# Linear attention with a routed MoE on one core: per-head q and k features by folded weights, or from one projection spread by DMA

## The reference

```python
h = _layernorm(x) * (1 + ca) + sa                 # ca, sa: from silu(c) @ wmod, per sequence
qkv = h @ w_qkv.T;  q, k, v = split(qkv)           # to blocks: [b, head, block, 32, 16]
qp = elu(einsum('bhcsd,hdf->bhcsf', q, proj)) + 1.0    # 16 -> 128 features
kp = elu(einsum('bhcsd,hdf->bhcsf', k, proj)) + 1.0
kv = einsum('bhcsf,bhcsd->bhcfd', kp, v)
num = einsum('bhcsf,bhcfd->bhcsd', qp, kv);  ksum = kp.sum(axis=3)
z = 1.0 / (einsum('bhcsf,bhcf->bhcs', qp, ksum) + 1e-08)
x = x + ga * ((num * z) @ w_out.T + b_out)
h = _layernorm(x) * (1 + cb) + sb
x = x + gb * ffn(h)       # best of 8 experts by a small gate: w1 128x512, gelu, w2 512x128, times its score
```

## Time and profile before

| | us |
|---|---|
| median of 3 runs | 293.38 (293.2 to 293.75) |
| profiled execution, first to last instruction | 292.5 |
| begin of the first head's `phi` | 15.3 |
| one steady step | 21.6 |
| last `phi` of the last step done | 189.1 |
| tail behind it | 103.4 |

### The profile page before, as it was taken

One profiled execution on the slowest core, in us unless ns is written; L12 is line 12 of the kernel. 1 busy time (PEld: TensorE's weight loads), 2 busy tenths in 40 slices (PEclk: granted clock), 3 DMA queues, 4 the chain that ended last, 5 costly groups with the idle time before them and its releaser, 6 DMA issues.

```text
span 292.5 us, 11379 instructions
## 1 busy us (share of the span) xinstructions
PE 264.7 (91%) x3952; PEld 212.3 (73%) x3953; DVE 233.8 (80%) x772; ACT 224.2 (77%) x516; POOL 166.2 (57%) x193
## 2 busy tenths in 40 slices
PE   8999799999999999999999999899686999999970
PEld 2566576678778777777777776678575999999960
DVE  3787969989999999999999989988884476676750
ACT  2589698999989989989989988856964667676740
POOL 7004154344476675675685681878788874454551
PEclk9999999999999999999999999999999999999996
DMA  5999800000001001001001011513355344444400
GB/s 149 286 358 300 199 3 2 2 4 4 2 29 56 30 29 56 31 29 57 29 29 56 29 45 70 163 58 113 126 168 176 117 126 123 112 126 131 117 28 0
DMA packets 16239, 26.13 MB, mean 89 GB/s; under 512 B 2608, under 2 KB 11060, under 8 KB 16193
## 3 DMA queue, kind: packets, MB, share of 16 engines
q1 hardware_dynamic: 12896, 17.10, 21.2%
q0 software_dynamic: 3296, 8.41, 8.0%
HBM read 15.32 MB, written 10.64 MB: 89 GB/s over the span
## 4 chain that ended last, share of the span: by engine, by line
PE 45%; DVE 20%; issue 8%; ACT 8%; POOL 5%; DMA 2%; POOLq 1%; ACTq 0%; DVEq 0%; SPq 0%
PE ps L885 9%; DVE phi L1179 8%; PE ps L913 8%; PE ps L810 6%; PE ps L812 4%; PE ps L811 4%; PE ps L821 3%; ACT ebuf L577 3%; ACT ebuf L581 2%; PE ps L843 2%; POOL sorted_rows L458 2%; DVE h L1248 2%; PE ps L835 2%; DVE ln_st L1231 2%; PE ps L879 1%
## 5 line engine op out<-in xcount | busy, mean ns | idle before, releaser
L1179 DVE SCALAR_TENSOR_TENSOR phi<-ps,ebuf 128x512 f32<-128x512 f32 x128 | 81.9, 680 | 13.2 <-ACT ebuf L581 13.1
L577 ACT ACTIVATE ebuf<-ps 128x1024 f32<-128x1024 f32 x64 | 65.5, 1024 | 15.5 <-PE ps L812 15.0
L581 ACT ACTIVATE ebuf<-ebuf 128x512 f32<-128x512 f32 x128 | 74.4, 636 | 0.1
L810 PE MATMUL ps<-hT_hi,mix_lo 128*128 128x512 f32 x128 | 58.4, 456 | 8.1 <-DVE phi L1179 4.5
L635 ACT ACTIVATE gT<-ps,b_cols 128x128 f32<-128x128 f32 x156 | 44.6, 367 | 17.1 <-PE ps L885 14.6
L812 PE MATMUL ps<-hT_hi,mix_hi 128*128 128x512 f32 x128 | 50.6, 396 | 0.0
L811 PE MATMUL ps<-hT_lo,mix_hi 128*128 128x512 f32 x128 | 50.6, 395 | 0.0
L913 PE MATMUL ps<-w_sb,gT 128*128 x312 | 42.3, 278 | 4.0 <-DVE y L1501 2.8
L913 PEld LDWEIGHTS ps<-w_sb,gT 128*128 128x128 f32 x312 | 37.9, 192 | 6.0 <-issue 5.9
L527 POOL DMA_INDIRECT out<-yo,tok x27 | 27.0, 1001 | 23.8 <-DVE yo L1517 21.9
L458 POOL DMA_INDIRECT sorted_rows<-rec,pos x32 | 32.6, 1017 | 8.4 <-issue 6.6
(11 more groups left out here) (208 smaller groups left out, 465.2 us busy)
## 6 DMA issues: line engine op xcount, KB each, us to landing
rin<-sorted_rows SPq DMA_DIRECT2D x39, 192.5 KB, 2.5
w1b<-in_L_ffn_w SPq DMA_DIRECT2D x1, 2048.0 KB, 14.2
sorted_rows<-pad_rec SPq DMA_DIRECT2D x9, 192.5 KB, 6.2
w1b<-in_L_ffn_b SPq DMA_DIRECT2D x1, 512.0 KB, 7.4
sorted_rows<-rec,pos POOLq DMA_INDIRECT x32, 3.1
out<-yo,tok POOLq DMA_INDIRECT x27
wmod_sb<-in_L_wmod SPq DMA_DIRECT2D x1, 384.0 KB, 4.0
x_all<-in_L_attn_x SPq DMA_DIRECT2D x1, 256.0 KB, 3.4
```

Source lines behind the costliest of these rows:

```text
L577: nc.scalar.activation(ebuf[:, h % 2, :, :], x_ps[h % 2], ACT.Relu, scale=-1.0).then_inc(s_neg, 1)
L581: nc.scalar.activation(ebuf[:, h % 2, j, :], ebuf[:, h % 2, j, :], ACT.Exp, scale=-1.0).then_inc(s_exp, 1)
L810: mm(x_ps[h % 2][:, j, :], mix_lo[:, j, h, :], hi, start=True, stop=False)
L1179: v.scalar_tensor_tensor(out=phi[:, h % 4, j, :], in0=x_ps[h % 2][:, j, :], scalar=0.0, in1=ebuf[:, h % 2, j, :], op0=ALU.max, op1=ALU.add ...
```

## The change

q and k of a group are projected once, by two fp32 products of 128 rows (`project`, PE), cast to a high part (`keep_hi`, ACT) and a low part (`split_lo`, now on DVE). Then DMAs on SP's queue (`feed_heads`) lay them out anew in `feed`: under each head its 16 rows of the high, low and again high part, and a row of ones, at partitions 0 to 48 for q and 64 to 112 for k. A head's features are then one product of 49 rows for each of q and k. The row of ones adds 1 to the feature, and everything is scaled by `SHRINK`, so that elu(x)+1 = max(x + 1, min(exp(x), 1)) takes one ACT and one DVE instruction of 1024 columns; the scale is taken out in `keep_a`. `vals` now has the column of ones itself, and four DMAs a group (`spread_values`) write the diagonal blocks of `vbd` instead of DVE. The additions to the variances go to POOL, and the first normalisation runs two groups ahead. The rest of x is loaded in two DMAs, ACT's queue loads `proj` in six; the expert weights are loaded two experts at a time in steps 1 to 4, the pads in step 1, the biases in step 2. The modulation rows are made before the first step. `feed` and `qk` have one buffer each.

```diff
 # SP
+            def feed_heads(g, half, j):
+                sp.wait_ge(s_lo, 2 * g + j + 1)
+                if g:
+                    sp.wait_ge(s_x, H * (g - 1) + HH * (half + 1))
+                for part, row in ((0, 0), (1, HD), (0, 2 * HD)):
+                    sp.dma_start(feed[2 * BLK * j + row:2 * BLK * j + row + HD, HH * half:HH * (half + 1), :].bitcast(F32),
+                                 qk[HH * HD * half:HH * HD * (half + 1), part, j, :].bitcast(F32)).then_inc(s_ld[half][j], 16)
...
+            def spread_values(g):
+                sp.wait_ge(s_vs, g + 1)
+                if g == 0:
+                    sp.wait_ge(c_vbd, 2)
+                else:
+                    sp.wait_ge(s_av, 2 * g)
+                for c in range(NC):
+                    sp.dma_start(vbd[c * BLK:(c + 1) * BLK, c, :],
+                                 vals[c * BLK:(c + 1) * BLK, :, :, :].rearrange("p t h w -> p (t h w)")).then_inc(s_vbd, 16)
...
+            for g in range(NG - 1):
+                if g:
+                    spread_values(g)
+                feed_heads(g + 1, 0, 0)
+                feed_heads(g + 1, 0, 1)
+                if 1 <= g <= E // 2:
+                    load_experts(2 * (g - 1))
+                if g == 1:
+                    sp.wait_ge(c_dve, 1)
+                    for e in range(E + 1):
+                        sp.dma_start(sorted_rows[e * REGION:e * REGION + P, :], pad_rec[:, :]).then_inc(s_tail, 16)
+                if g == 2:
...
+                feed_heads(g + 1, 1, 0)
+                feed_heads(g + 1, 1, 1)
+            spread_values(NG - 1)
 # ACT
-                nc.scalar.activation(ebuf[:, h % 2, :, :], x_ps[h % 2], ACT.Relu, scale=-1.0).then_inc(s_neg, 1)
-                between()
-                act.wait_ge(s_neg, H * g + h + 1)
-                for j in range(2):
-                    nc.scalar.activation(ebuf[:, h % 2, j, :], ebuf[:, h % 2, j, :], ACT.Exp, scale=-1.0).then_inc(s_exp, 1)
+                nc.scalar.activation(ebuf[:, h % 2, :, :], x_ps[h % 2], ACT.Exp, scale=1.0 / SHRINK,
+                                     bias=math.log(SHRINK) - 1.0).then_inc(s_exp, 1)
+
+            def keep_hi(g, j, first=False):
+                act.wait_ge(s_qk, 2 * g + j + 1)
+                if not first:
+                    for half in range(2):
+                        act.wait_ge(s_ld[half][j], 48 * g)
+                nc.scalar.copy(qk[:, 0, j, :], t_ps).then_inc(s_hi, 1)
 # PE
+            def project(g, j):
+                if j == 0:
+                    pe.wait_ge(s_ht, g + 1)
+                else:
+                    pe.wait_ge(s_lo, 2 * g + 1)
...
+                mm(t_ps, wqkT[:, j, :], hT[:, :], start=True, stop=True).then_inc(s_qk, 1)
...
+                for j in range(2):
+                    rows = slice(2 * BLK * j, 2 * BLK * j + 3 * HD + 1)
+                    last = mm(x_ps[h % 2][:, j, :], proj_k[rows, h, :], feed[rows, h, :], start=True, stop=True)
+                last.then_inc(s_x, 1)
 # DVE
+            def split_lo(g, j):
+                dve.wait_ge(s_hi, 2 * g + j + 1)
+                v.tensor_tensor(qk[:, 1, j, :], t_ps, qk[:, 0, j, :].bitcast(F32), ALU.subtract).then_inc(s_lo, 1)
...
-                for j in range(2):
-                    dve.wait_ge(s_exp, 2 * (H * g + h) + j + 1)
-                    v.scalar_tensor_tensor(out=phi[:, h % 4, j, :], in0=x_ps[h % 2][:, j, :], scalar=0.0,
-                                           in1=ebuf[:, h % 2, j, :], op0=ALU.max, op1=ALU.add).then_inc(s_phi, 1)
+                dve.wait_ge(s_exp, H * g + h + 1)
+                v.scalar_tensor_tensor(out=phi[:, h % 4, :, :], in0=ebuf[:, h % 2, :, :], scalar=SHRINK,
+                                       in1=x_ps[h % 2], op0=ALU.min, op1=ALU.max).then_inc(s_phi, 1)
```

## The result

The changed kernel takes 326.75 us (324.75 to 327.43, 4 runs) where the kernel before took 293.29 beside it: a ratio of 1.113, 95% interval 1.109 to 1.116. The range, 273 to 307, missed it by 20 us, and the sign was wrong. The profiled execution has a span of 325.1 us, 32.6 more than before.

A forecast was written before the change was run, and what follows sets the result against it. PE, DVE and ACT were nearly level (20.9, 20.1, 19.6 of 21.6 us a step); after the change the feeds' loop would bind. Steps end at 186.0, plus tail 103.4: span 289.4, forecast 290 us, range 273 to 307.

The forecast's parts named there:

- What each engine loses: Busy time per step: PE from 20.9 to 15.4 us, ACT 19.6 to 11.5, DVE 20.1 to 17.4.
- The loop: Eight steps: next q cast waits for the running group's q feeds; period 17.5 us plus other queue work.
- X(g+1) = X(g) + 11.9 + 6c: Landing of a group's last feed, from the previous group's: 11.9 us plus six feeds, plus whatever else is queued.
- c: Time one 128 KB feed takes in SP's queue: taken as 0.93 us, between ends of 0.45 and 2.8.
- The sign that I had given for a c over 1.1: ACT idle behind head 1, before the cast of q, for over 4 us in steps 5 and 6.
- The queue's other work: Between feed halves: expert loads 3.2 us a step in steps 1 to 4, pads 7.0, b2 2.0, scatters 1.2.
- the sum: Landings of last feeds added group by group, from X(0) 26.0 to X(7) 175.1 us; steps end at 186.0.
- b1 would hold the queue: Step 2: the little b1 load was counted as nothing, but up to 10 us if its issue time is its own.
- The start: Before the first step: split of k ends at 15.65, first phi at 22.2 against 15.29, losing 7 us.
- The tail, held to be unchanged: Stretch behind the eight steps: stays 103.4 us.
- The clock: Rival: PE's clock falls to 1.2 GHz; one fall in step 1 costs 1 us, half of each step about 320; chance 0.05.
- feeds hidden: Rival: c from 0.45 to 0.75, DVE's 18.2 us sets the steps, 276 us (273 to 283); chance 0.26.

The follow-up runs named there:

- early: double2 with k of the next group projected and cast behind head 3 instead of 4, split behind head 3 instead of 5: 301.7 us.
- double2: Kernel after with a second buffer for qk, so the cast waits for the feeds of the group before last: 321.8 us.
- stride: Kernel after with the rows of feed reordered, each feed writing every third of 48 partitions instead of 16 in a row: 313.7 us, ratio 1.066.
- thin: Kernel after with each feed of groups 1 to 7 moving 64 of 512 columns, attention not the reference's: 305.4 us.
- Experiment 8: Kernel after with first hT made before ACT waits for proj, fillers, and one modulation product less between the first projections: 325.5 us.
- best: Kernel after with stride's rows, early's buffers and split, later expert loads, 20 fillers a step, earlier first hT: 288.3 us, ratio 0.983.
- fill: Kernel after with filler products on PE from group 1: 12 at head 0, 6 at head 4, 2 at other heads: 335.3 us.
- fill0: Kernel after with 14 filler products on PE at head 0 alone of each step from group 1: 329.1 us.
- es_start: Kernel after with the edits of early and stride together and the start of Experiment 8: 295.0 us, ratio 1.002.
- es_fill: es_start with 20 filler products a step on PE, 4 at heads 0 and 4, 2 at the others: 293.0 us, ratio 0.997.

## Why the prediction was wrong, point by point

- **What each engine loses** held. PE was forecast 15.4 us a step; it had 15.1 in step 6 of early at a clock of 1.00, and up to 20.5 where the clock was 0.72. DVE came to 17.9 for 17.4 and ACT to 12.8 for 11.5: I had taken ACT's lines, whose durations overlap (all of them add up to 22.0 in that step), from the window's 19.6, in which they do not. `phi` of 1024 columns took 1.14 us from start to start, as forecast.
- **The loop** was the step that failed, and it cost most: from the first `phi` to the end of the steps the forecast has 163.8 us (22.2 to 186.0), and they took 191.3. I saw that the cast of q waits for the q feeds of the running group, and wrote X(g+1) = X(g) + 11.9 + 6c, with the cast free to go when these had landed. I left out what stands ahead of the cast on its own engine: the exponentials of heads 0 and 1 of the running group, which need the *k* feeds of half 0, their products and the scores. The circle through head 0 is, in its own terms, 11.2 + 6.4 + 2.1 + 4.8 = 24.5 us. My 11.9 + 6c, at c = 1.08 and with 1.2 for the scatters, gives 19.6. Most of the difference is the way from k's split to the next cast: I had six feeds and their landing, 6c + 2.0 or 8.5, and over head 0 it took 6.4 + 2.1 + 4.8 = 13.3. double2 showed that the wait I had built on was worth 5 us, though it did bind in steps 2 to 5; early showed that k's place late in the step was worth 20 more. The sign that I had given for a c over 1.1, ACT idle for over 4 us at the cast in steps 5 and 6, did not come (1.07 us and none), rightly, and yet the steps were long.
- **What c is.** I took 0.93, an eighth of the wide rate and three feeds side by side. It was 1.08, 121 GB/s with the engines at a share of 1.07; no run tells one feed alone from three, so how far they overlap stays open. The Trainium skill's figure ("SBUF — State Buffer", section "Door 1: The DMA port swizzle"), which I quoted against the change, made an estimated 1.26, too much by 0.18, but its rule on partitions is what stride then bore out. By my own formula 0.15 us of c is 7 us; by thin the whole transfer is 21 us.
- **The queue's other work** was priced about right where it was largest: it is issued in step 1 and holds back group 2's second half, so it shows in step 2: 31.1 us, 7 more than the steps without loads, against 9 in the sum. In steps 3 and 4 it shows with 1 us, for 3 to 4 forecast. That b1 would hold the queue was ruled out: SP issued it in 0.50 us.
- **The start** was forecast to lose 7 us and lost 11.8. These rows show where. ACT waited for the six loads of `proj` before it made `hT`:

```profile
10.59 1.04 ACT L628 CAST proj_k<-proj_bd 128x1024 fp32r<-128x1024 f32 x1 [4.15 <-DMA proj_bd<-in_L_attn_proj]
11.54 0.77 ACT L659 ACTIVATE hT<-ps,modT 128x512 f32<-128x512 f32 x1
```

PE, idle before, made the first projection at half clock (2.08) and then two modulation products (3.35), where I had 1.0 and 0.8:

```profile
12.37 2.08 PE L841 MATMUL ps<-hT,wqkT 128*128 128x512 f32 x2 [3.43 <-ACT hT L659]
14.23 3.35 PE L849 MATMUL ps<-wmod_sb,o_sb 128*128 128x512 f32 x4
...
25.46 0.50 PE L876 MATMUL ps<-feed,proj_k 49*128 49x512 f32 x2 [2.74 <-issue]
```

The split of k ended at 19.8 in place of 15.65, and the feeds landed 5.7 us after it, for 4.8. Experiment 8 took away the first of these and gave most of it back by its fillers. best, with these mended, has its first `phi` at 22.9, near the forecast's 22.2, though with the faster feeds of stride. The tail, held to be unchanged, was 3.3 longer; that is in the next point.

- **The clock.** I gave it 5% and one microsecond. It did fall, in nearly every step, to the lower level of 1.2 GHz. Yet fill and fill0 found no gain, and with the loop open (es_start, es_fill) steps 3 to 6 took 19.8 to 20.4 us at a clock of 0.69 to 0.84 and 20.2 to 20.5 at 1.00. What the clock does cost is in the tail and where the circle passes PE, some 2 us of the link to the next cast: the tail took 106.7 us in the kernel after and 105.4 to 107.5 in the runs without fillers, but 101.8 to 104.7 in fill, fill0, es_fill and best. What the kernel after would take at full clock without fillers in its way was not measured.
- **The rival "feeds hidden"** would not have given 276 us either (its terms add up to 276.8). With the loop open and the clock full, a step takes 20.2 us, not 18.2. DVE works 17.7 of it; ACT's exponentials wait for products, and DVE for them. Taking the sum of an engine's work plus 0.8 for the length of a step, in a circle over three engines, was two microseconds short.

How much of the last point is the pace PE, ACT and DVE give each other and how much the fillers themselves (20 a step, an estimated 4.3 us of PE) was not parted.

## What to carry to other kernels

When work is moved to a new path (here: projection, cast, split, DMA, product), write down the whole circle from a step's product back to itself, with every instruction that stands *ahead* of each link on its own in-order engine, and add the times round it: buffers and placement, not the busy sums, set the step. Issue what feeds the next group's transfer as early in the step as its inputs allow; moving one split two heads forward and its projection and cast one (with a second buffer) was worth 25 us here, more than taking away seven-eighths of the feeds' bytes, 21. And before spreading data by DMA, see which partitions each transfer writes: the same 16 rows laid every third partition went 1.4 times as fast in a full queue. When fillers are to hold PE's clock, see what stands behind them: eight of them cost the start 1.8 us.

## What the runs showed of the hardware

In a full queue feeds on 16 neighbouring partitions moved 121 GB/s and feeds on every third of 48 partitions 167; loads over all 128 partitions reached 371. The DMA engines showed nearly the same share in all three cases (1.07, 1.07 and 1.06), so that "DMA busy" says nothing of bytes. SP started a feed of 128 KB every 0.64 us, which caps such feeds at an estimated 205 GB/s, and 205 was seen where the queue was not full. A feed of 16 KB landed 2.3 us after its issue, one of 128 KB 3.9 (medians, three in a row). Of the clock: before, one pause of 2.4 us, in a stretch with PE nearly idle, had left it at 1.00; here, with one or two pauses of 2.1 to 6.8 us in each of steps 1 to 6 and PE at 15 to 20 us of steps of 18 to 31, the mean in a step was 0.58 to 0.90. Why it was at 0.58 in step 0, which has no such pause in it, is not shown.
